# A language-model layer on one core: the router's product folded into the projection, and another opening

## The chip, the core and the metric

One Trainium2 core runs the whole program in one launch. It has five instruction streams: TensorE (PE, matrix products into PSUM), VectorE (DVE), ScalarE (ACT), GpSimd (POOL) and SyncE (SP, which here issues DMAs), all in order, each waiting on semaphores that the others or the DMAs raise. The metric is the device time of one execution in microseconds (us).

## The reference

128 sequences of 128 tokens, width 128. The layer is one embedding, one attention and one mixture of experts:

```python
nesting, segments = _syntax_info(token_ids)
combined = concat([pos_emb, nest_table[nesting], seg_table[segments]])   # [b, s, 384]
h = combined @ W                                                         # width 128
h = h + attention(layernorm(h))       # 8 heads of 64, causal inside the 128 tokens, biases on q, k, v, o
x2 = layernorm(h)
logits = x2 @ router_w.T + router_b   # 8 experts
top 2 of logits, softmax over the two -> weights
h = h + sum over the two experts of weight * (fc2(silu(h1) * h2) + b)    # h1, h2 = split(x2 @ fc1 + b), 2 * 256
```

Positions come from a table, and nesting and segment codes from comparisons and running sums over the token ids. The layer norms have no scale or shift.

## The kernel before

**Stages.** An opening loads the weights, computes codes from the token ids, writes them to DRAM and reads them back spread over 72 partitions, builds a table of embeddings (`code_table`), splits the projection weights into a high part and a rest (`w_hi`, `w_lo`) and prepares two groups of four sequences. Then sixteen octets of eight sequences run attention and routing, software-pipelined: in each turn k of an octet (one sequence), `octet_steps` lists the steps that every engine then works off in the same order, each engine picking the kinds it has a part in. The last octet is followed by `last_steps`, which drains the routing of the last groups. The rows of all tokens are scattered to DRAM by expert, and an expert phase in blocks of 256 rows follows, once for the first choice and once for the second.

**A turn.** With n = k mod 4 the turn holds: scores (L1113), a query, a value and a key product for the next group, each as three products of high and low parts (L1050 to L1052), softmax (mask and row maximum on DVE L809 and L813, exponentials on ACT L640 in two halves of four heads, scaling of one half on POOL L497 and of the other on DVE L826), transposes of the probabilities (L1120, L1125), mix with the values (L1137) and projection (L1147), whose result DVE adds to `residual` as `h2` (L837). The embedding (n=0, L1065), its norm and transposes (n=1, n=2) of the group two ahead are put between.

**Routing of a group, over four turns.** DVE takes statistics of `h2` (n=2) and writes the normalised rows `normed2` (n=3, L857). In the n=0 turn PE transposes the rows (L1155) and ACT copies them to `x2T` (L632); in n=1 PE multiplies them with `w_router` (L1164, 8 columns), DVE adds the bias (L863) and takes the two largest; n=2 makes one-hots of the choices; n=3 ranks them (L1172, L1173); n=0 turns ranks into row numbers, and POOL scatters (L529) in n=0 and n=1. The PSUM banks KEY and VALUE are shared by these steps with the key and value products, so the next product waits until they have been read out.

**The opening's order.** SP first raises all counting semaphores by 64 (so that waits can count backwards), then issues x, the embedding tables, wq, wk, wv, their biases, wo, the two halves of the expert weights w1 (1 MB each, into the still unused `kT[1]` and `qT[1]`), w2, the router's weight, b2 and b1, and only then waits for the codes and stores them. `first_steps` does embedding, norm and transposes of group 0, then of group 1, then query, value and key of group 0 four times. Before the first octet ACT casts both halves of w1 (L663) and DVE computes their rest (L994); ACT waits for that rest before it goes on.

## Time and profile before

| what | value |
|---|---|
| median of 3 runs | 1486.12 us (1485.44 to 1490.86) |
| profiled execution | 1479.45 us, span 1477.7 us |
| PE, DVE, ACT, POOL busy over the span | 88%, 81%, 72%, 60% |
| granted TensorE clock, mean | 0.973 |
| opening, to the first scores | 0 to 60 us |
| attention with routing | 60 to 1042 us |
| expert phase | 1050 to 1478 us |

The shares are averages over stages with different limits. A row of the chain of waits gives the start, the length and the work that the end of the program hangs on at that time; a row of the windows gives for each engine how long it was busy in that stretch. Idle time of an engine that nothing waits for costs nothing.

### The profile page before, as it was taken

To read this page: it belongs to the slowest core of one execution; us is meant where nothing else is said; L and a number is where in the kernel's file an instruction comes from. 1 tells how busy PE (TensorE), PEld (TensorE's weight loads), DVE (VectorE), ACT (ScalarE), POOL (GpSimd) and SP (SyncE) were. 2 spreads that over 40 slices of the span, in tenths; PEclk is the share of its full clock that TensorE was granted. 3 is DMA by queue.
4 is the path that set the end of the run, shared out by engine and by line. 5 is a ranking of instruction groups with operands and counts; after the bars stand their busy time and mean duration, and the time that the engine had idled before them with its cause. 6 is when DMAs were issued, how large, how long until landed. Compare 5 with 4: busy or idle time off the path is not lost.

```text
span 1477.7 us, 42129 instructions
## 1 busy us (share of the span) xinstructions
PE 1300.5 (88%) x11234; PEld 1128.5 (76%) x11235; DVE 1195.4 (81%) x3683; ACT 1057.6 (72%) x3382; POOL 889.5 (60%) x1161
## 2 busy tenths in 40 slices
PE   1699999999999999999999999993399999699996
PEld 0488777777777777777777777773399999699996
DVE  4478888888888888888888888884588888588885
ACT  0599888888888888888888888882255555355553
POOL 3134566656665666566656665666366767477775
PEclk9999999999999999999999999996699999899998
DMA  4042111101110111011101110111789999899995
GB/s 150 3 175 79 33 46 39 40 31 45 38 40 31 45 38 40 31 45 38 40 31 45 38 40 31 45 38 57 248 306 343 345 337 340 278 335 346 338 348 187
DMA packets 91501, 188.43 MB, mean 128 GB/s; under 512 B 18404, under 2 KB 38588, under 8 KB 90812
## 3 DMA queue, kind: packets, MB, share of 16 engines
q1 hardware_dynamic: 50748, 66.35, 14.7%
q10 hardware_dynamic: 20864, 76.87, 13.6%
q0 software_dynamic: 19840, 44.62, 8.6%
q8 instruction: 23, 0.38, 0.1%
q14 instruction: 26, 0.21, 0.1%
HBM read 50.40 MB, written 57.44 MB: 73 GB/s over the span
## 4 chain that ended last, share of the span: by engine, by line
PE 33%; DVE 19%; issue 16%; ACT 12%; DMA 10%; POOL 6%; SPq 2%; DVEq 1%; ACTq 0%; POOLq 0%
ACT probs L640 6%; PE ps L1137 6%; PE ps L1147 4%; PE ps L1050 3%; DMA v<-xs 3%; ACT v L627 3%; PE ps L1052 3%; PE ps L1051 3%; DVE neg_max L813 3%; PE ps L1202 3%; DVE masked L809 3%; DVE probsT L817 2%; ACT qT L618 2%; PE ps L1164 2%; PE ps L1120 2%
## 5 line engine op out<-in xcount | busy, mean ns | idle before, releaser
L640 ACT ACTIVATE probs<-masked,neg_max 128x128 f32<-128x128 f32 x1024 | 398.5, 393 | 9.9 <-DVE neg_max L813 8.0
L529 POOL DMA_INDIRECT xs<-normed,row x256 | 266.1, 1039 | 79.7 <-issue 72.4
L497 POOL TENSOR_TENSOR probs<-probs,inv_sums 128x512 f32<-128x512 f32 x128 | 133.0, 1039 | 268.0 <-DVE inv_sums L821 267.9
L640 ACT ACTIVATION_READ_ACCUMULATOR probs<-masked,neg_max 128x1 f32 x1024 | 193.8, 189 | 0.0
L809 DVE TENSOR_TENSOR masked<-ps,causal 128x1024 f32<-128x1024 f32 x128 | 155.7, 1216 | 37.7 <-PE ps L1113 36.1
L1050 PE MATMUL ps<-xT_hi,w_now 128*128 128x256 f32 x576 | 178.8, 310 | 6.8 <-issue 6.1
L1137 PE MATMUL ps<-probsT,v 128*64 128x128 f32 x2048 | 140.2, 277 | 35.2 <-DVE probsT L817 35.2
L594 ACT ACTIVATE masked<-ps,w_now 128x256 f32<-128x256 f32 x288 | 120.7, 470 | 65.0 <-PE ps L1052 55.1
L1051 PE MATMUL ps<-xT_lo,w_now 128*128 128x256 f32 x576 | 163.3, 283 | 0.0
L1052 PE MATMUL ps<-xT_hi,w_now 128*128 128x256 f32 x576 | 163.2, 283 | 0.0
L986 DVE SCALAR_TENSOR_TENSOR probsT<-ps,w_now,masked 128x256 f32<-128x256 f32 x288 | 126.1, 480 | 41.7 <-PE ps L1052 21.6
L1202 PE MATMUL ps<-w,probsT 128*128 x1152 | 152.2, 275 | 3.6 <-DVE probsT L986 3.6
L813 DVE TENSOR_REDUCE neg_max<-masked 128x8 f32<-128x1024 f32 x128 | 154.9, 1210 | 0.0
L1137 PEld LDWEIGHTS ps<-probsT,v 128*64 128x64 f32 x2048 | 113.0, 137 | 54.8 <-issue 45.5
L1113 PE MATMUL ps<-kT,qT 64*128 64x128 f32 x2048 | 149.7, 286 | 0.8 <-ACT kT L621 0.8
L1202 PEld LDWEIGHTS ps<-w,probsT 128*128 128x128 f32 x1152 | 141.1, 192 | 4.2 <-issue 4.2
L1113 PEld LDWEIGHTS ps<-kT,qT 64*128 64x128 f32 x2048 | 125.0, 188 | 22.9 <-issue 21.7
L563 POOL DMA_INDIRECT xs<-probs,v x108 | 104.9, 971 | 61.2 <-DVE probs L967 31.2
L1147 PE MATMUL ps<-w_o,mixedT 128*128 128x128 f32 x1024 | 136.2, 276 | 0.0
L563 POOL DMA_INDIRECT out_h<-probs,v x108 | 104.5, 968 | 51.9 <-issue 28.2
L578 ACT CAST xT_hi<-ps 128x256 fp32r<-128x256 f32 x144 | 53.6, 372 | 103.4 <-PE ps L1182 100.8
L1147 PEld LDWEIGHTS ps<-w_o,mixedT 128*128 128x128 f32 x1024 | 125.3, 193 | 0.0
(190 smaller groups left out, 3264.9 us busy)
## 6 DMA issues: line engine op xcount, KB each, us to landing
w_now<-w_parts ACTq DMA_DIRECT2D x144, 514.0 KB
v<-xs SPq DMA_DIRECT2D x108, 260.0 KB
kT<-xs SPq DMA_DIRECT2D x36, 260.0 KB
normed<-h SPq DMA_DIRECT2D x32, 256.0 KB, 2.6
pads<-pad_rows SPq DMA_DIRECT2D x8, 520.0 KB, 2.8
xs<-pad_rows SPq DMA_DIRECT2D x8, 520.0 KB, 3.6
xs<-normed,row POOLq DMA_INDIRECT x256, 2.4
xs<-pads SPq DMA_DIRECT2D x12, 260.0 KB
```

The lines of the kernel that those rows point to most:

```text
L529: pool.indirect_dma_start((xs[0], xs_parts)[k], bass.IndirectOffsetOnAxis(ap=row[par][:, k, j:j + 1].bitcast(U32), axis=0), normed2[par][: ...
L563: pool.indirect_dma_start((xs_parts, out)[k], bass.IndirectOffsetOnAxis(ap=xt[j][:, r, GOES_TO[k]:GOES_TO[k] + 1].bitcast(U32), axis=0), y ...
L640: ins = nc.scalar.activation(probs[par][:, n], masked[par][:, n], ACT.Exp, bias=neg_max[par][:, n:n + 1], scale=1.0, accum_out=sums[par][: ...
L809: V.tensor_tensor(masked[par][:], ps[:, SCORES:SCORES + 2].rearrange("p a (n k) -> p (a n) k", n=4), causal[:].unsqueeze(1).broadcast_to([ ...
L813: V.tensor_reduce(neg_max[par][:], masked[par][:], AX, ALU.max, negate=True).then_inc(max_ready, 1)
L1050: T.matmul(dst, w_hi_, x_hi_, start=True, stop=False)
L1051: T.matmul(dst, w_hi_, x_lo_, start=False, stop=False)
L1052: return T.matmul(dst, w_lo_, x_hi_, start=False, stop=True)
L1113: ins = T.matmul(ps[:, SCORES + e, pair * S:(pair + 1) * S], qT[gp][rows, pair, cols], kT[gp][rows, pair, cols], start=True, stop=True)
L1137: ins = T.matmul(ps[e * HD:(e + 1) * HD, MIX, pair * S:(pair + 1) * S], v[gp][:, j, head * HD:(head + 1) * HD], probsT[:, e * PAIRS + pair ...
L1147: ins = T.matmul(ps[:, QUERY, 0:D], mixedT[:, n], w_o[:, n], start=(n == 0), stop=(n == PAIRS - 1))
L1202: ins = T.matmul(ps[:, YB[z], r * D:(r + 1) * D], actT[z][:, half, r * S:(r + 1) * S], w2[:, bass.ds(e * 2 * D + half * D, D)], start=(hal ...
```

## The change

Two edits that share tiles.

**The router's product.** Let w_c be the router's weight with the mean over the 128 features taken off (`centre` @ `w_router`). Then the router's logits of a row are rstd times (h2 @ w_c) plus the bias. h2 is linear in table rows, mixed values and biases, so w_c is multiplied into the embedding weights, `w_o` and the output bias once, as 8 more columns (D2 = 136). `code_table`, `pos_emb`, `w_o`, `bias_o`, `h`, `residual` and `h2` get 136 columns. The projection then yields the raw logits with no product of their own; the embedding gets a second narrow product (`embed_r`, n=1). The steps `route_normT` and `route_logits` go; in the n=3 turn DVE scales the raw logits by rstd and adds the bias.

**The opening.** The semaphores are raised by PE and ACT, half each. SP issues x, the router's weight, transposed copies of W and wo, the tables and the projection weights, then the codes. ACT issues w1 first thing, and b1, the router bias, w2 and b2 after its cast of `w_hi`. DVE makes `part_code` and `part_mask` ahead of the codes. `first_steps` weaves group 1's embedding, norm and transposes between the query, value and key products of group 0. The cast of w1 moves to ACT's part of the eight turns of octet 0 and its rest to POOL's part of octet 1.

```diff
             steps.append(("embed", half + 2))
         elif n == 1:
-            late("route_logits", half - 2)
+            steps.append(("embed_r", half + 2))
...
-            late("route_normT", half - 2)
             steps.append(("stats", half + 2))
             late("route_rows", half - 3)
         elif n == 1:
@@ -98,6 +98,9 @@
             steps.append(("residual", half + 1))
         if octets_done == 0:
             steps.extend(("pad", n) for n in ((2 * k, 2 * k + 1) if k < GB else (GB + k,)))
+            steps.append(("w1_hi", k))
+        if octets_done == 1:
+            steps.append(("w1_lo", k))
...
-            [(w, 0, n) for n in range(PAIRS) for w in ("query", "value", "key")])
+    steps = [(w, 0) for w in ("onehot", "embed", "embed_r", "stats", "rstd")] + [("split", 0), ("onehot", 1)]
+    steps += [(w, 0) for w in ("norm", "normT", "xlo")] + [("bias", 0)]
+    between = {0: [("embed", 1)], 1: [("embed_r", 1)], 2: [("normT", 1)], 3: []}
+    behind = {0: [("stats", 1), ("rstd", 1)], 1: [("norm", 1)], 2: [("xlo", 1)], 3: [("onehot", 2), ("residual", 0)]}
+    for n in range(PAIRS):
+        steps += [(w, 0, n) for w in ("query", "value", "key")] + between[n] + behind[n]
```

SP's loads, POOL's and ACT's share, the router's steps on DVE, and PE's opening with the narrow product:

```diff
-            for s in led:
-                sp.sem_inc(s, LEAD)
             sp.dma_start(x_raw[:], a["x"]).then_inc(s_x, 16)
+            sp.dma_start(w_router[:], a["wr"]).then_inc(s_wr, 16)
+            sp.dma_start(w_embT[:], a["w_embT"]).then_inc(s_wrT, 16)
+            sp.dma_start(w_oT[:], a["woT"]).then_inc(s_wrT, 16)
+            sp.dma_start(bias_oT[:], a["boT"]).then_inc(s_wr, 16)
...
             sp.dma_start(bias_vT[:], a["bv"]).then_inc(s_wqkv, 16)
-            sp.dma_start(bias_o[:], a["bo"].broadcast_to([128, D])).then_inc(s_wqkv, 16)
-            sp.dma_start(w_o[:], a["wo"].rearrange("(c p) n -> p c n", c=PAIRS)).then_inc(s_wqkv, 16)
-            sp.dma_start(w1_raw[0][:].rearrange("p a b -> p (a b)"), a["w1"][:, 0:EXPERTS * FC1 // 2]).then_inc(s_w1, 16)
-            sp.dma_start(w1_raw[1][:].rearrange("p a b -> p (a b)"), a["w1"][:, EXPERTS * FC1 // 2:]).then_inc(s_w1, 16)
-            sp.dma_start(w2[:], a["w2"]).then_inc(s_w1, 16)
-            sp.dma_start(w_router[:], a["wr"]).then_inc(s_w1, 16)
-            sp.dma_start(bias_r[:], a["br"].broadcast_to([S, EXPERTS])).then_inc(s_w1, 16)
-            sp.dma_start(b2_all[:], a["b2"].broadcast_to([S, EXPERTS * D])).then_inc(s_w1, 16)
-            sp.dma_start(b1_all[:].rearrange("p e c -> p (e c)"), a["b1"]).then_inc(s_b1, 16)
+            sp.dma_start(bias_o[:, 0:D], a["bo"].broadcast_to([128, D])).then_inc(s_wqkv, 16)
+            sp.dma_start(w_o[:, :, 0:D], a["wo"].rearrange("(c p) n -> p c n", c=PAIRS)).then_inc(s_wqkv, 16)
...
+                elif kind == "w1_lo":
+                    pool.wait_ge(s_w1hi, i + 1)
+                    pool.tensor_tensor(w1_parts[:, i, FC1:2 * FC1], w1_parts[:, i, FC1:2 * FC1].bitcast(F32),
+                                       w1_parts[:, i, 0:FC1].bitcast(F32), ALU.subtract).then_inc(s_w1lo, 1)
...
+            for s in led[0::2]:
+                act.sem_inc(s, LEAD)
+            act.dma_start(w1_parts[:, :, FC1:2 * FC1].bitcast(F32), a["w1"].rearrange("p (e c) -> p e c", e=EXPERTS)).then_inc(s_w1, 16)
+            act.wait_ge(s_ext_ps, 1)
+            act.wait_ge(s_w, 16 * 4)
+            nc.scalar.copy(w_emb[:, :, D:D2], ps[:, KEY, EXPERTS:4 * EXPERTS].rearrange("p (c e) -> p c e", c=3)).then_inc(s_ext, 1)
+            nc.scalar.copy(w_o[:, :, D:D2], ps[:, KEY, 4 * EXPERTS:8 * EXPERTS].rearrange("p (c e) -> p c e", c=PAIRS)).then_inc(s_ext, 1)
             act.wait_ge(s_wqkv, 16 * 8)
             nc.scalar.mul(bias_q8[:], bias_qk[:, 0], HD ** -0.5).then_inc(s_whi, 1)
             nc.scalar.copy(w_hi[:], w_raw[:]).then_inc(s_whi, 1)
+            act.dma_start(w1_parts[:, :, 2 * FC1:W1ROW].bitcast(F32), a["b1"].rearrange("p (e c) -> p e c", e=EXPERTS)).then_inc(s_b1, 16)
+            act.dma_start(bias_r[:], a["br"].broadcast_to([S, EXPERTS])).then_inc(s_w2, 16)
+            act.dma_start(w2[:], a["w2"]).then_inc(s_w2, 16)
+            act.dma_start(b2_all[:], a["b2"].broadcast_to([S, EXPERTS * D])).then_inc(s_w2, 16)
...
+                elif kind == "embed_r":
+                    dve.wait_ge(embed_r_full, LEAD + G + 1)
+                    V.tensor_tensor(h[par][:, :, D:D2], ps[:, VALUE, 0:GB * EXPERTS].rearrange("p (j e) -> p j e", j=GB),
+                                    pos_emb[:, D:D2].unsqueeze(1).broadcast_to([S, GB, EXPERTS]), ALU.add).then_inc(embedded_r, 1)
...
-                    dve.wait_ge(x2T_full, LEAD + G - 1)
+                    V.tensor_tensor(raw[:], h2[par][:, :, D:D2], rstd2[:].unsqueeze(2).broadcast_to([S, GB, EXPERTS]), ALU.mult).then_inc(raw_ready, 1)
...
-                    dve.wait_ge(logits_full, LEAD + G + 1)
+                    dve.wait_ge(raw_ready, LEAD + G + 1)
                     dve.wait_ge(top_at_ready, LEAD + G)
-                    V.tensor_tensor(logits[:], ps[:, VALUE, 0:GB * EXPERTS].rearrange("p (j e) -> p j e", j=GB),
+                    V.tensor_tensor(logits[:], raw[:],
                                     bias_r[:].unsqueeze(1).broadcast_to([S, GB, EXPERTS]), ALU.add).then_inc(logits_ready, 1)
...
+            for s in led[1::2]:
+                pe.sem_inc(s, LEAD)
+            pe.wait_ge(s_centre, 1)
+            pe.wait_ge(s_wr, 32)
+            T.matmul(ps[:, KEY, 0:EXPERTS], centre[:], w_router[:], start=True, stop=True).then_inc(s_wc_ps, 1)
+            pe.wait_ge(s_wc, 1)
+            pe.wait_ge(s_wrT, 32)
+            for c in range(3):
+                T.matmul(ps[:, KEY, (1 + c) * EXPERTS:(2 + c) * EXPERTS], w_embT[:, c * 128:(c + 1) * 128], w_c[:], start=True, stop=True)
+            for c in range(PAIRS):
+                ins = T.matmul(ps[:, KEY, (4 + c) * EXPERTS:(5 + c) * EXPERTS], w_oT[:, c * 128:(c + 1) * 128], w_c[:], start=True, stop=True)
+            ins.then_inc(s_ext_ps, 1)
             pe.wait_ge(s_w, 16 * 4)
-            T.matmul(ps[:, VALUE, 0:D], posT[:], w_emb[:, 0], start=True, stop=True, skip_group_check=True)
-            T.matmul(ps[0:CODES, VALUE, D:2 * D], nestT[:], w_emb[:, 1], start=False, stop=False, skip_group_check=True)
-            T.matmul(ps[0:CODES, VALUE, D:2 * D], segT[:], w_emb[:, 2], start=False, stop=True, skip_group_check=True).then_inc(s_table_ps, 1)
+            pe.wait_ge(s_ext, 1)
+            T.matmul(ps[:, VALUE, 0:D2], posT[:], w_emb[:, 0], start=True, stop=True, skip_group_check=True)
+            T.matmul(ps[0:CODES, VALUE, D2:2 * D2], nestT[:], w_emb[:, 1], start=False, stop=False, skip_group_check=True)
+            T.matmul(ps[0:CODES, VALUE, D2:2 * D2], segT[:], w_emb[:, 2], start=False, stop=True, skip_group_check=True).then_inc(s_table_ps, 1)
+            pe.wait_ge(s_bias_v, 1)
+            pe.wait_ge(s_ext, 2)
+            pe.wait_ge(s_wc, 2)
+            for n in range(PAIRS):
+                T.matmul(ps[:, MIX, 0:D2], bias_v[:, n], w_o[:, n], start=(n == 0), stop=False)
+            T.matmul(ps[:, MIX, D:D2], bias_oTs[:], w_c[:], start=False, stop=True).then_inc(s_bias_o_ps, 1)
...
+                elif kind == "embed_r":
+                    if first:
+                        pe.wait_ge(embedded, LEAD + G + 1)
+                    else:
+                        pe.wait_ge(v_ready, LEAD + GB * (G - 1) + 2)
+                    for j in range(GB):
+                        ins = T.matmul(ps[:, VALUE, j * EXPERTS:(j + 1) * EXPERTS], onehot[:, j * S:(j + 1) * S], code_table[:, D:D2],
+                                       start=True, stop=True)
+                    ins.then_inc(embed_r_full, 1)
```

Value products wait for the woven steps:

```diff
                 elif kind == "value":
...
                     elif j == 1:
                         pe.wait_ge(embedded, LEAD + G + 2)
                     elif j == 2:
-                        pe.wait_ge(logits_ready, LEAD + G - 2)
+                        pe.wait_ge(embedded_r, LEAD + G + 2)
                     else:
                         pe.wait_ge(xlo_ready, LEAD + G + 2)
```

Where instructions stand. PE, from right behind an n=0 turn's mix of probabilities and values into the n=1 turn (scores, nine products of query, value and key, the step behind them), before:

```order
L1155 MATMUL ps<-ident,normed_0 128x128 x4
L1113 MATMUL ps<-kT,qT 128x128 x8
L1050 MATMUL ps<-xT_hi,w_hi 128x512
L1051 MATMUL ps<-xT_lo,w_hi 128x512
L1052 MATMUL ps<-xT_hi,w_lo 128x512
L1050 MATMUL ps<-w_hi,xT_hi 128x512
L1051 MATMUL ps<-w_lo,xT_hi 128x512
L1052 MATMUL ps<-w_hi,xT_lo 128x512
L1050 MATMUL ps<-xT_hi,w_hi 128x512
L1051 MATMUL ps<-xT_lo,w_hi 128x512
L1052 MATMUL ps<-xT_hi,w_lo 128x512
L1164 MATMUL ps<-w_router,x2T 128x8 x4
```

and now, from the mix (`ps<-probsT,v`) on:

```order
L1180 MATMUL ps<-probsT,v 64x128 x8
L1156 MATMUL ps<-kT,qT 128x128 x8
L1085 MATMUL ps<-xT_hi,w_hi 128x512
L1086 MATMUL ps<-xT_lo,w_hi 128x512
L1087 MATMUL ps<-xT_hi,w_lo 128x512
L1085 MATMUL ps<-w_hi,xT_hi 128x512
L1086 MATMUL ps<-w_lo,xT_hi 128x512
L1087 MATMUL ps<-w_hi,xT_lo 128x512
L1085 MATMUL ps<-xT_hi,w_hi 128x512
L1086 MATMUL ps<-xT_lo,w_hi 128x512
L1087 MATMUL ps<-xT_hi,w_lo 128x512
L1109 MATMUL ps<-code_table,onehot 128x8 x4
```

The transposes L1155 ahead of the scores are gone, and the router's product L1164 behind the value and key products has become four narrow products of table and one-hot.

DVE in the n=3 turn, from the copy of the ranks to the maximum of the next turn (`gap_one` and `normed` behind it are the routing weights), before:

```order
L902 COPY ranks<-ps 128x128
L817 COPY probsT<-ps 128x512
L837 TENSOR_TENSOR h_0<-ps,residual 128x128
L779 TENSOR_SCALAR onehot<-code_rows,part_code 72x512
L857 TENSOR_SCALAR normed_1<-h_1,moments,rstd 128x128 x4
L894 TENSOR_SCALAR gap_one<-gap_exp 128x4
L896 RECIPROCAL normed_0<-gap_one 128x4
L898 TENSOR_TENSOR normed_0<-gap_exp,normed_0 128x4
L821 RECIPROCAL inv_sums<-sums 128x4
L809 TENSOR_TENSOR masked<-ps,causal 128x1024
```

and now:

```order
L927 COPY ranks<-ps 128x128
L843 COPY probsT<-ps 128x512
L863 TENSOR_TENSOR h_0<-ps,residual 128x136
L795 TENSOR_SCALAR onehot<-code_rows,part_code 72x512
L881 TENSOR_TENSOR raw<-h_1,rstd 128x32
L883 TENSOR_SCALAR normed_1<-h_1,moments,rstd 128x128 x4
L888 TENSOR_TENSOR logits<-raw,bias_r 128x32
L919 TENSOR_SCALAR gap_one<-gap_exp 128x4
L921 RECIPROCAL normed_0<-gap_one 128x4
L923 TENSOR_TENSOR normed_0<-gap_exp,normed_0 128x4
L847 RECIPROCAL inv_sums<-sums 128x4
L835 TENSOR_TENSOR masked<-ps,causal 128x1024
```

Two operations of 32 columns stand on either side of the four norms; the bias add was behind the n=1 turn's maximum before.

SP's loads at the start, from wo (`w_o`) to the first codes that come back, before:

```order
L330 DMA w_o<-in_wo 128x4x128
L331 DMA kT<-in_w 128x2048
L332 DMA qT<-in_w 128x2048
L333 DMA w<-in_w 128x2048
L334 DMA w_router<-in_wr 128x8
L335 DMA bias_r<-in_br 128x8
L336 DMA b_all<-in_b 128x1024
L337 DMA b_all<-in_b 128x32
L340 DMA codes<-v 128x2x128
L341 DMA codes<-v 16x2x128
L347 DMA code_rows<-codes 48x512
```

and now:

```order
L339 DMA bias_o<-in_bo 128x128
L340 DMA w_o<-in_wo 128x4x128
L343 DMA codes<-v 128x2x128
L344 DMA codes<-v 16x2x128
L350 DMA code_rows<-codes 48x512
```

The seven loads between wo and the store of the codes are gone from this queue.

## Rows read from the trace of the kernel before

Columns of the windows: stretch, length, then busy us and count for PE, PEld, DVE, ACT and POOL, the granted clock, the DMA share and GB/s.

**Rows 1.** Windows of one steady group: us, then PE, PEld, DVE, ACT, POOL busy, clock, DMA.
```profile
300.25:307.63 7.38, 7.33 (x66) 6.15 (x65) 5.37 (x14) 6.19 (x22) 5.53 (x7) 1.00 0.10 36
...
321.63:329.84 8.21, 7.23 (x68) 5.87 (x66) 7.80 (x24) 6.70 (x22) 3.00 (x6) 1.00 0.00 0
300.25:329.84 29.59, 28.01 (x252) 23.09 (x251) 25.82 (x82) 25.78 (x88) 18.45 (x25) 1.00 0.12 38
```

**Rows 2.** Windows, first octet: the group of sequences 4 to 7, and its n=1 turn.
```profile
89.54:115.80 26.26, 25.93 (x239) 21.82 (x237) 21.82 (x53) 24.55 (x85) 10.97 (x22) 1.00 0.48 179
...
96.50:102.72 6.22, 6.22 (x60) 5.34 (x58) 5.18 (x14) 5.97 (x21) 3.29 (x7) 1.00 0.35 131
```

**Rows 3.** Groups by line and shape, 300 to 420 us: busy us, mean ns | idle before.
```profile
L497 POOL TENSOR_TENSOR probs<-probs,inv_sums 128x512 f32<-128x512 f32 x17 | 17.7, 1039 | 35.7 <-DVE inv_sums L821 35.7
...
L1147 PE MATMUL ps<-w_o,mixedT 128*128 128x128 f32 x128 | 16.9, 275 | 0.0
...
L1164 PE MATMUL ps<-w_router,x2T 128*128 128x8 f32 x32 | 4.2, 259 | 0.2
...
L632 ACT COPY x2T<-ps 128x512 f32<-128x512 f32 x5 | 2.9, 585 | 0.2
...
L1065 PE MATMUL ps<-code_table,onehot 72*128 72x128 bf16 x16 | 1.6, 221 | 0.5
...
L863 DVE TENSOR_TENSOR logits<-ps,bias_r 128x32 f32<-128x32 f32 x4 | 0.8, 192 | 0.9 <-PE ps L1164 0.9
```

**Rows 4.** Chain that ended last, steady group: start, us, what.
```profile
313.80 0.17 DVE h L837
...
328.23 1.09 PE ps L1137 x16
329.32 0.60 PE ps L1155 x4
...
330.42 1.55 ACT probs L640 x7
...
333.34 1.06 PE ps L1164 x8
```

**Rows 5.** The same chain over the opening.
```profile
6.78 1.15 SPq L319
...
19.09 10.12 DMA codes<-v
...
31.47 0.36 DVE onehot L779
...
39.86 0.35 DVE onehot L779
...
49.33 0.80 PE ps L1050
...
60.06 1.16 PE ps L1113 x16
...
64.04 2.28 DVE w_parts L994
66.33 1.15 DVE masked L809
```

**Rows 6.** Timeline of the opening: start, us, instruction [idle before, releaser].
```profile
9.54 0.23 DVE L719 CAST v<-v 128x128 f32<-128x128 int32 x1 [9.54 <-DMA v<-in_x]
...
14.83 0.23 DVE L735 CAST v<-v 128x128 bf16<-128x128 int32 x1
...
36.31 1.12 DVE L800 TENSOR_SCALAR normed<-h,moments,rstd 128x128 f32<-128x128 f32 x4 [1.60 <-POOL rstd L468]
...
59.91 1.89 ACT L663 CAST w_parts<-kT 128x2048 fp32r<-128x2048 f32 x1
```

**Rows 7.** The chain again, behind attention.
```profile
1009.54 1.09 POOL xs L529
...
1041.91 7.67 DMA xs<-normed,row
```

176 lines of the change are left out of this document (77 added, 99 removed).

## The prediction

> **What bounds the kernel now.** I read the table of windows first, because the busy shares of the whole span mix an opening, sixteen octets of attention and an expert phase. One steady group of four sequences takes 29.59 us; in it TensorE is busy 28.01 us, VectorE 25.82 and ScalarE 25.78 [rows 1]. A turn (one sequence) with little idle on TensorE is the n=1 turn, 7.33 of 7.38 us; in the n=0 turn VectorE is the full one, 7.80 of 8.21, and TensorE has a microsecond of idle time in it. A group of the first octet, which has no router transposes, products, ranks or scatters yet, takes 26.26 us [rows 2]: routing costs 3.33 us a group, and that is the ceiling of anything won from it.
>
> Next the chain of waits through a steady group. From 313.80 to the mix product at 328.23 it is VectorE's almost without a gap (some forty pieces, one stretch of POOL among them), then on TensorE and ScalarE: mix, the router's transposes (L1155), ScalarE's exponentials at 330.42, the value copy, the router's product (L1164) [rows 4]. So both of TensorE's router steps stand on the chain; the VectorE half of the chain is full, and whatever is added there lengthens it.
>
> Then the opening, as the chain of the first 70 us [rows 5]. SyncE's first DMA is issued at 6.78, behind its semaphore increments. The codes are ready at 15.06 [rows 6], but their two stores stand behind all weight loads; the second is issued at 19.09 and has landed 10.12 us later. The first one-hot starts at 31.47, the first query product at 49.33 (two groups prepared one behind the other), the first scores at 60.06. VectorE splits the expert weights until 66.3 and takes the scores only then. Everything up to there is nearly pure latency: a microsecond taken off is one microsecond of the end.
>
> Last the tail. After attention the chain is POOL's: a row of scatters from 1009.54, then the last landing at 1041.91 [rows 7]. The last two groups' router steps lie under those scatters, so I give the change nothing there. The expert phase behind it runs the same instructions on the same weights: nothing either.
>
> **The router's fold, per steady group.** Removed from TensorE on the chain: the transposes, 0.60 us [rows 4]. ScalarE's copy of the transposed rows (0.585 [rows 3]) goes too, but the mixedT copy of about the same length runs beside the transposes, so only one of the two lengths is won: from the end of mix at 329.32 the exponentials can start after one copy, at about 329.85 in place of 330.42 [rows 4], 0.57 us. The product goes, 4.2 us over four groups, 1.05 a group; the new narrow product of one-hot and table's last 8 columns takes its place, and its nearest row is the same product at 128 columns, 1.6 over four groups, 0.40 [rows 3]: 0.65 us won. Fewer columns are not worth less time here: the router's own product has 8 columns and 259 ns, the projection 128 columns and 275 [rows 3]. Together 1.22.
>
> Added: two small VectorE operations (scaling the raw logits by rstd, and the bias add, which moves from the n=1 turn) in the n=3 turn, inside the full half of the chain. The bias add is 192 ns [rows 3]; two of them are 0.38 at most, and 0.1 at least, since small operations overlap in issue. I take 0.30. The new add from PSUM in the n=1 turn replaces the old bias add of the same size: nothing. The projection gets 8 more columns: 16.9 us over 128 instructions (each two passes and 16 sequences) [rows 3], so at most 8/128 of 1.06 us, 0.07 a sequence, at least nothing; four times, on the chain for two of four turns: 0 to 0.14, taken 0.10. The wider residual and h2 adds: 8/128 of small operations, 0.05. Net 1.22 - 0.30 - 0.10 - 0.05 = 0.77 us a group, bounds 0.4 (all additions full, some of the win filled by VectorE) and 1.25. Both router steps occur for 30 groups before the tail: **23 us, 12 to 38**.
>
> **The opening.** Semaphore increments leave SyncE, so x is issued at about 0.4 instead of 6.78, lands some 2.8 us later (9.54 against 6.78 [rows 5, 6]), but VectorE first waits for the router's folded weight: constants from POOL, five DMAs (20 issues took from 7.93 to 19.09, so 0.56 us each), their landing, one product: done at about 6.9. The code computation takes 5.5 us (9.54 to 15.06 [rows 6]): codes at 12.5. SyncE has by then issued its 17 loads (the first 1.15 us, the rest 0.56 each, done near 10.5) and issues the second store at 13.1, not 19.09. What the store costs is the open point: 10.12 us before with 3.5 MB of weights ahead in its queue [rows 5]. Now the 2 MB of w1 is issued by ScalarE at about 3.6 us and should be through by 13, and w2 and b2 (1.5 MB) are issued after the store. Lower bound 2.5 us for the store (x took 2.8), upper bound the old 10. I take 3, since little is left in flight, then 2.3 for the loads (29.21 to 31.47 before): first one-hot at **18.5**, between 17.5 and 22 (the ends are 2.5 and some 6.5 us of store; the full 10 is a rival). The table chain on VectorE ends near 16 and is covered.
>
> From one-hot to the first query was 8.5 us for one group (31.47 to 39.9, the second group used 39.9 to 49.33 [rows 5]). Now 0.95 more for the narrow product and its add ahead of the statistics, and 0.55 because the weight split (1536 columns, where 2048 take 2.28 [rows 5]: 1.7) and the next one-hot (0.35) are put into the 1.60 us in which VectorE waited for POOL's rstd [rows 6]: 10.0 us. The query block took 10.7 (49.33 to 60.06). With the second group woven in, value 1 waits for the embed add (0.9), value 2 for the narrow add and the transposes for the norm (about 0.6), value 3 for the low part of x (1.5): 13.7, between 12 and 15.5. First scores at 18.5 + 10.0 + 13.7 = 42.2, not 60.06: 17.8 won. The stall behind the expert split, 66.33 against 61.2 where the scores ended, goes: 4.5 (3.2 to 5.5; the low end if TensorE's own work in the first two turns is what is late next).
>
> Given back: eight ScalarE casts of 128x512 in octet 0, a quarter each of the 1.89 us row [rows 6], 0.47; ScalarE is nearly full there (24.55 of 26.26 [rows 2]), so between 0 and 0.47 a turn: 2.5 in all (0 to 4). POOL's eight subtractions in octet 1, near 1.04 each like the 128x512 product [rows 3], beside idle time of POOL: 0.5 (0 to 2). The narrow product in octet 0, where TensorE is full: 0.5. Opening: 17.8 + 4.5 - 2.5 - 0.5 - 0.5 = **18.8 us, 11 to 26**.
>
> **Sum.** 18.8 + 23.1 = 41.9 us off the profiled execution's own 1479.45, which gives 1437.5. The runs shown have their median 6.7 us higher, at 1486.12; taken off that, 1444.2. I forecast 1444.
>
> **A rule against a row.** For the store, the table of the opening shows that a DMA behind 3.5 MB on one queue lands after 10.12 us. The Trainium skill (DMA: Bandwidth & Descriptors, Issuing engines are not separate DMA queues) says DMAs issued by several engines run on the same 16 engines and interleave, so issuing w1 from ScalarE saves only sequencer time. By the rule the codes still share bandwidth with w1 and w2; the sum would be 3 to 4 us smaller. No run here shows it yet.
>
> **Rivals.** (A) VectorE takes over as the bound. VectorE has 25.82 us of work and gets 0.4 more; its chain half is already without gaps. If its backlog fills what TensorE gives up, the fold is worth 0 to 0.3 us a group and only the opening stays: 1486 - 19 - 5 = 1462. For it: the 14 us without a gap. Against it: 3.77 us of VectorE idle in each group, 2.01 of them in turn n=1 [rows 1], where the larger win falls. The Trainium skill (Perfetto Trace Analysis, Identifying the Most-Contended Engine) says to judge TensorE by weight-load busy share, not by matmuls; that is 23.09 us a group here, below VectorE's, and the rule speaks for this rival. (B) Both steps pay in full and the VectorE additions hide: 1.25 a group, 38 us, with the opening 57: 1429. (C) The codes still queue: the store lands as late after its issue as before, first one-hot at 25, opening 12 rather than 19: 1451 with the fold. (D) Slower: the additions on VectorE (0.38), the narrow product (0.40), its add (0.19) and the wide columns (0.28 over four turns) are paid in full, 1.25 us a group on 32 groups, 40 us, while the removed steps were only fillers of waits for VectorE. With the opening that is 1486 + 40 - 19 = 1507. It decides from the point where the n=1 and n=0 turns do not shrink and the group passes 30.2 us. Against it: the n=1 turn has TensorE at 99%, and the same turn without router steps took 6.22 us in octet 0 [rows 2]. (E) The change does not do what it says at the opening (VectorE waits at the router weight or the full load of q, k, v until after the codes are there): part of C.
>
> **Chances.** Forecast 0.55 (1434 to 1454 is its own range); A 0.17; B 0.13; C with E 0.11; D 0.04. The range should hold 8 in 10: from 1422 (B with a good opening) to 1464 (A). The measurement tells 0.5%, 7.4 us, from no change. Faster by more: everything but D and the poorest part of A, 0.93; within: 0.04; slower: 0.03.
>
> **What would show it.** First one-hot near 18.5 and first scores near 42; no wait of VectorE's mask for the expert split. Steady group near 28.8 us, n=1 near 6.7, n=0 near 7.7, n=3 about 0.3 longer. The n=1 turn of octet 0 some 0.5 longer than 6.22. Wrong if the store takes over 6 us, if a steady group is still above 29.3 or below 28.3, or if the expert phase changes its length.

## The result and the profile after

The changed kernel takes **1444.02 us** (median of four runs, 1441.04 to 1446.21) beside 1487.19 for the kernel before (four runs, 1485.44 to 1490.86) on the same chip: a ratio of 0.9705 with the 95% interval 0.9677 to 0.9733. Its profiled execution took 1442.6 us, span 1440.8. Repeated later in another session it took 1441.25 us beside 1485.13, ratio 0.971 [0.9694, 0.9726].

The forecast was 1444. Its parts were not as good as its sum, and the rest of this text is about that. The table cuts the span at four points that both traces show: the first scores, the scores of the ninth sequence (behind the first octet), the scores of the last sequence, and the first transpose of the expert phase. All in us.

| stretch | before (three profiles) | after (two profiles) | difference of the means |
|---|---|---|---|
| start to first scores | 60.06, 61.39, 59.49 | 48.53, 47.36 | -12.4 |
| first two turns | 16.40, 15.71, 16.45 | 11.95, 11.92 | -4.3 |
| other six turns of the octet | 39.34, 39.38, 39.32 | 41.88, 41.90 | +2.5 |
| the next 120 turns | 878.09, 878.24, 877.86 | 846.07, 846.22 | -31.9 |
| last scores to expert phase | 60.77, 60.39, 60.27 | 60.64, 60.74 | +0.2 |
| expert phase | 423.0, 428.8, 433.4 | 431.7, 428.6 | +1.7 |

The 120 turns repeat within 0.4 us and the six turns within 0.1; the very start moves by a microsecond or two with the first loads. The expert phase is the same program in both kernels and scatters by 10 us from execution to execution. So small effects can be read from the cut points and not from the end. In the first two turns the kernel before also has a lower granted clock (0.79, 0.89 and 0.79, against 1.00 in both profiles after), so a part of the -4.3 came through the clock.

Windows of the changed kernel: the first two turns, the other six of the first octet, then an n=1 turn, an n=0 turn and the whole of a steady group. The columns are those of [rows 1, 2].

```profile
48.53:60.48 11.95, 9.40 (x83) 7.23 (x83) 9.52 (x23) 9.32 (x32) 2.62 (x6) 1.00 0.12 45
60.48:102.36 41.88, 39.61 (x360) 32.94 (x358) 31.77 (x72) 39.40 (x134) 12.97 (x32) 1.00 0.44 162
280.76:287.34 6.58, 6.51 (x63) 5.36 (x62) 5.72 (x19) 6.12 (x21) 4.74 (x5) 1.00 0.06 20
301.36:309.28 7.92, 6.89 (x63) 5.46 (x62) 7.66 (x20) 6.21 (x21) 3.07 (x6) 1.00 0.00 0
280.76:309.28 28.52, 26.91 (x244) 21.93 (x243) 26.67 (x83) 25.23 (x86) 18.89 (x25) 1.00 0.12 40
```

Against [rows 1] the n=1 turn went from 7.38 to 6.58 us, the n=0 turn from 8.21 to 7.92, the group from 29.59 to 28.52. Over all 120 turns the mean n=1 turn went from 7.38 to 6.58, n=0 from 8.21 to 7.80, n=2 from 6.93 to 7.15 and n=3 from 6.98 to 6.91. TensorE works 1.10 us less in a group, VectorE 0.85 more: VectorE now has 26.67 of 28.52. The lengths of most groups alternate in both kernels (29.43 and 29.62 before, 28.32 and 28.47 after), on the mean of the two 29.53 and 28.40.

The chain through the steady group, to be laid beside [rows 4]: the router's raw product and its scaling on VectorE (L881, L888), mix (L1180), the exponentials, the narrow product (L1109), the projection (L1190).

```profile
300.77 0.18 DVE raw L881
...
302.02 0.10 DVE logits L888
...
308.26 1.11 PE ps L1180 x16
...
309.87 1.54 ACT probs L656 x7
...
312.78 0.26 PE ps L1109 x4
...
313.96 0.93 PE ps L1190 x8
```

From the start of mix to the exponentials it is 1.61 us, where it was 2.19 [rows 4]: the transposes are gone and one copy is left. Between the value copy and the attention's transposes stands a product of 0.26 us, where the router's took 1.06. In return 0.18 and 0.10 us of VectorE are on the chain.

By line and shape, 280 to 395 us, the answer to [rows 3]:

```profile
L1190 PE MATMUL ps<-w_o,mixedT 128*128 128x136 f32 x128 | 17.5, 279 | 0.0
...
L1109 PE MATMUL ps<-code_table,onehot 72*128 72x8 bf16 x16 | 1.0, 169 | 0.3
...
L881 DVE TENSOR_TENSOR raw<-h,rstd 128x32 f32<-128x32 f32 x4 | 0.7, 180 | 0.0
L888 DVE TENSOR_TENSOR logits<-raw,bias_r 128x32 f32<-128x32 f32 x4 | 0.7, 178 | 0.0
```

The opening's chain, to be laid beside [rows 5]. "issue" is time in which the trace shows nothing that is waited for.

```profile
2.67 2.63 DMA v<-in_boT
5.30 2.87 issue
8.17 0.58 PE ps L1061 x2
...
8.85 0.17 DVE w_c L749
...
15.00 3.68 DMA codes<-v
...
19.09 4.01 DMA code_rows<-codes
...
23.29 0.36 DVE onehot L795
...
33.78 0.76 PE ps L1085
```

The last of the constants is there at 5.30, but TensorE's first product starts at 8.17: it is still issuing its half of the semaphore increments. The codes are ready at 14.54, the second store is issued at 15.00 and lands in 3.68 us, where it took 10.12 [rows 5]; their loads take 4.01, where they took 1.66 in the trace of before. From the store's landing to the first one-hot, the issue of the loads included, it is 4.61 us, where it was 2.26. First one-hot 23.29 (31.47 before), first query product 33.78 (49.33), first scores 48.53 (60.06). The mask behind the first scores no longer waits for a split of expert weights, as it did from 61.2 to 66.33 [rows 5].

### The profile page after: what moved, and what is told of

It reads as the page before. It is cut to its first block, busy times and chain, and to the rows that moved or that the text cites. A ratio compares the mean times of both kernels' runs of the same rounds, so it can differ in the third digit from the quotient of the medians.

```text
span 1440.8 us, 41566 instructions
## 1 busy us (share of the span) xinstructions
PE 1269.9 (88%) x11004; PEld 1093.6 (76%) x11005; DVE 1206.8 (84%) x3749; ACT 1039.4 (72%) x3358; POOL 906.6 (63%) x1171
## 4 chain that ended last, share of the span: by engine, by line
PE 31%; issue 19%; DVE 18%; ACT 14%; DMA 8%; POOL 8%; SPq 1%; DVEq 0%; POOLq 0%; ACTq 0%
ACT probs L656 7%; PE ps L1180 6%; PE ps L1190 4%; DVE neg_max L839 4%; PE ps L1085 3%; ACT v L648 3%; ACT qT L639 3%; PE ps L1227 3%; DMA v<-xs 3%; PE ps L1087 3%; PE ps L1086 3%; PE ps L1163 2%; DVE probsT L843 2%; POOL xs L537 2%; PE ps L1168 2%
## 5 line engine op out<-in xcount | busy, mean ns | idle before, releaser
L537 POOL DMA_INDIRECT xs<-normed,row x256 | 260.2, 1016 | 79.7 <-issue 68.3
L835 DVE TENSOR_TENSOR masked<-ps,causal 128x1024 f32<-128x1024 f32 x128 | 155.7, 1216 | 23.3 <-PE ps L1156 10.9
L1180 PE MATMUL ps<-probsT,v 128*64 128x128 f32 x2048 | 140.9, 279 | 32.2 <-DVE probsT L843 29.1
L1180 PEld LDWEIGHTS ps<-probsT,v 128*64 128x64 f32 x2048 | 113.0, 137 | 52.4 <-issue 46.1
L1190 PE MATMUL ps<-w_o,mixedT 128*128 128x136 f32 x1024 | 141.8, 282 | 0.8 <-ACT mixedT L676 0.8
L1190 PEld LDWEIGHTS ps<-w_o,mixedT 128*128 128x128 f32 x1024 | 129.4, 192 | 1.1 <-issue 1.1
```

The source lines that it names most:

```text
L537: pool.indirect_dma_start((xs[0], xs_parts)[k], bass.IndirectOffsetOnAxis(ap=row[par][:, k, j:j + 1].bitcast(U32), axis=0), normed2[par][: ...
L835: V.tensor_tensor(masked[par][:], ps[:, SCORES:SCORES + 2].rearrange("p a (n k) -> p (a n) k", n=4), causal[:].unsqueeze(1).broadcast_to([ ...
L1180: ins = T.matmul(ps[e * HD:(e + 1) * HD, MIX, pair * S:(pair + 1) * S], v[gp][:, j, head * HD:(head + 1) * HD], probsT[:, e * PAIRS + pair ...
L1190: ins = T.matmul(ps[:, QUERY, 0:D2], mixedT[:, n], w_o[:, n], start=(n == 0), stop=(n == PAIRS - 1))
```

## The experiments

Twelve kernels ran. Seven undo or add one thing in the changed kernel, one combines four of them, one takes its whole opening back, and three are the two kernels themselves again. Four of them (incs_pool, w2_later, split_early, logits_n1) went to another chip, on which the kernel before takes 1669.64 us; more on it under logits_n1. The times of these four are not compared with the first chip's, only their openings, with logits_n1 as the base, since that one leaves the opening as it is.

### The fold without the opening

The old opening comes back (SyncE raises the semaphores, big weights ahead of the codes, groups one behind the other, expert weights split ahead of the octets):

```diff
+            for s in led:
+                sp.sem_inc(s, LEAD)
...
+            sp.dma_start(w1_parts[...], a["w1"]...).then_inc(s_w1, 16)   # and b1, br, w2, b2, ahead of the codes
...
-            act.dma_start(w1_parts[...], a["w1"]...).then_inc(s_w1, 16)
...
-    between = {0: [("embed", 1)], 1: [("embed_r", 1)], 2: [("normT", 1)], 3: []}
+    steps += [(w, 1) for w in ("embed", "embed_r", "stats", "rstd", "norm", "normT", "xlo")] + ...
```

> The fold kept, the old opening put back: semaphores raised by SyncE, all expert loads on SyncE ahead of the codes, group 1 behind group 0, expert weights split before the first octet (the fold's own small loads and products stay). If the steady saving is the fold's, the groups stay near 28.4 us and the time is that of before less 30 to 34 us, 1454 to 1457, with the first scores near 61 us. If the steady saving came with the other opening (other addresses, transfers or phase), the groups go back toward 29.5 us and the time is above 1475.

Measured: 1460.18 us (1453.88 to 1460.74) beside 1484.59, ratio 0.9823 [0.9791, 0.9856], 3 us above what was expected. Windows of the opening and of the 120 turns:

```profile
0.00:66.52 66.52, 22.42 (x93) 18.01 (x94) 23.06 (x86) 12.18 (x21) 17.25 (x50) 1.00 0.30 91
123.97:970.32 846.35, 799.69 (x7203) 652.50 (x7201) 777.31 (x2432) 751.58 (x2558) 544.55 (x732) 1.00 0.12 41
```

The 120 turns take 846.35 us, as in the changed kernel (846.07, 846.22), so the whole -31.9 is the fold's and none of it the opening's. The opening alone shows something that the sum had not priced whole: with the fold and the old order the first scores come at 66.52, 6 us later than before and 5.5 later than expected. The first one-hot is at 34.99 (31.47), since SyncE's queue reaches the second store at 24.39 instead of 19.09: one issue in it, that of the router bias behind w1 and b1, lasts 5.89 us (at most 0.97 for any issue between x and the store in the kernel before). So this opening is not quite the old one. From the one-hot to the query are 20.07 us, where it was 17.86: in each group 0.44 for the narrow product and its add (1.16 from the add of the embedding to the statistics, where it was 0.72), and 1.3 where GpSimd's var_eps runs beside the weight split (more under split_early). To the ninth sequence it is 123.97 us, 8.2 more than before: of the fold's 31.9 us, 24 are left in the whole kernel with this opening. With the new opening the ninth sequence comes at 101.2 to 102.4.

### The kernel before, again

> The kernel before, unchanged, profiled once more. The profiled execution of before had 423.0 us from the first transpose of the expert phase to the end, that of after 430.6, with the same instructions. If this is scatter from one execution to the next, this profile shows an expert phase that differs from 423.0 by several us, while its attention stage agrees with the first profile within 1 us (60.1 to 993.9). If the change lengthened the expert phase, this one is within 1.5 us of 423.0.

1485.8 us, span 1483.9, 6 us longer than the first profile. The expert phase starts at 1055.11 (1054.66 in the first), the first scores being 1.3 us later and the first two turns 0.7 shorter; the expert phase itself took 428.8 us instead of 423.0. That is the scatter of the table.

### Big weights ahead of the codes on SyncE's queue

```diff
+            sp.dma_start(w1_parts[...], a["w1"]...); b1; bias_r; w2; b2     # SyncE, behind all its other loads
...
-            act.dma_start(...)                                              # the same five on ScalarE
```

> The changed kernel with w1, b1, router bias, w2 and b2 issued by SyncE ahead of the store of the codes, nothing else undone. If the place in the queue is what made the store slow before, the landing of the store goes from 3.7 us back to about 10 and the first one-hot from 23.3 to 28 to 30 us. If only bytes in flight count and not the queue, the weights are through by the time of the store and the one-hot stays at 22 to 24.

1446.97 us in one run. Its opening chain:

```profile
10.36 5.50 SPq L343
...
17.32 7.56 DMA codes<-v
...
25.28 1.75 DMA code_rows<-codes
...
27.23 0.36 DVE onehot L795
```

The second store is issued at 17.32, not 15.00, and lands in 7.56 us, not 3.68: 6.2 us together, of which 2.3 come back because nothing is in flight beside the codes' loads (1.75, not 4.01). The later issue is not the price of five more issues: one of them, the router bias (L343), holds SyncE for 5.50 us, where the same issue on ScalarE takes 0.68 behind a landed w1; why is not shown. First one-hot 27.23, 3.9 us later than in the changed kernel's first profile (5.4 than in its second) and somewhat less than expected.

What this run does not separate is the queue from the bytes in flight. The weights were not through by the time of the store, as the second half of the expectation needed: w1 was issued at 8.89 and landed at 19.45 (4.20 and 16.55 in the changed kernel), and w2 and b2 were issued at 15.90 and 16.37, ahead of the store (18.94 and 19.41, behind it, in the changed kernel), and landed at 21.92 and 24.46. With w1 on ScalarE's queue a store issued earlier, at 12.99, took 4.23 us (incs_pool) and 4.92 (all_new), where one at 15.00 took 3.40 to 4.01. Big loads issued later and ahead of the store would explain the 7.56 on any queue.

### The second group not woven in

```diff
-    between = {0: [("embed", 1)], 1: [("embed_r", 1)], 2: [("normT", 1)], 3: []}
-    behind = {0: [("stats", 1), ("rstd", 1)], 1: [("norm", 1)], 2: [("xlo", 1)], 3: [("onehot", 2), ("residual", 0)]}
+    steps += [(w, 1) for w in ("embed", "embed_r", "stats", "rstd", "norm", "normT", "xlo")] + [("onehot", 2), ("residual", 0)]
```

> The changed kernel with group 1's embedding, norm and transposes put back ahead of the query, value and key products of group 0. The prediction priced the weaving at 9.4 us of a second group saved against 3.0 of waits put into the products. If so the first scores move from 48.5 to 54 to 55.5 us. If the woven steps cost the products as much as they saved, they stay within 2 us of 48.5.

1452.07 us in one run. First one-hot 21.96, first scores 53.31: 31.35 us between them, where the changed kernel has 25.24 and, in its second profile, 25.56. The first scores are a little ahead of what was expected, because the one-hot was 1.3 us earlier; from one-hot to scores the weaving is worth 5.8 to 6.1 us, and the terms of the sum give 6.4 (9.4 for the second group, less 3.0 for the longer block).

### TensorE's increments on GpSimd

```diff
+            for s in led[1::2]:
+                pool.sem_inc(s, LEAD)
...
-            for s in led[1::2]:
-                pe.sem_inc(s, LEAD)
```

> The changed kernel with TensorE's half of the semaphore increments moved to POOL behind its constants. In the profile TensorE's first product starts at 8.14 us although the last load it needs had landed at 5.3. If its own increments held it, it starts at 5.4 to 6 now, the codes are ready some 2.5 us earlier (near 12) and the first one-hot starts 1.5 to 2.8 us earlier than 23.3. If another wait held it, the product stays near 8.1.

The opening chain of this kernel (the other chip; logits_n1 there has 8.16, 14.99 and 22.18 at the same three places):

```profile
5.48 0.58 PE ps L1061 x2
...
12.99 4.23 DMA codes<-v
...
20.34 0.36 DVE onehot L797
```

The first product starts right behind the last constant, the codes' store is issued 2.0 us earlier, and the first one-hot comes 1.8 earlier. So the 2.87 us of "issue" in the changed kernel's chain were TensorE's own increments.

### Small weights behind the first codes

```diff
+            act.wait_ge(codes_in[0], LEAD + 32)
+            act.wait_ge(codes_in[1], LEAD + 32)
             act.dma_start(w1_parts[:, :, 2 * FC1:W1ROW]...)      # b1, then br, w2, b2
```

> The changed kernel with b1, router bias, w2 and b2 issued only when the first two loads of codes are in. If w2 and b2 in flight made the loads of the codes take 4.0 us instead of the 1.7 of before, the first one-hot moves from 23.3 to 20.5 to 21.5 us. If the load's time is its own, it stays within 0.5 us.

```profile
15.00 4.00 DMA codes<-v
...
19.41 1.66 DMA code_rows<-codes
...
21.26 0.36 DVE onehot L797
```

The store is unchanged (4.00), the loads take 1.66 us. With w2 and b2 (1.5 MB from ScalarE's queue) in flight the same loads took 2.34 to 4.16 us in the seven traces that have them (2.82 in logits_n1), so what it won here is 0.9 us of the first one-hot (22.18 in logits_n1) and up to 2.5 elsewhere. A queue of its own did not keep these small loads from a big one.

### The low half of the weights, earlier

```diff
-                elif kind == "split":
-                    V.tensor_tensor(w_lo[:], w_raw[:], w_hi[:].bitcast(F32), ALU.subtract)
...
+            V.tensor_tensor(w_lo[:], ...)          # ahead of the first one-hot
```

> The changed kernel with the rest of the projection weights computed on VectorE while it waits for the codes, not between group 0's statistics and norm. POOL's first operation of rstd took 1.53 us beside that split, 0.24 without it. If the split slows POOL, that operation is back at 0.24 and the span from one-hot to the first query product shrinks from 10.5 to 9.0 to 9.4 us. If the split is hidden there, the span stays within 0.3 of 10.5.

First one-hot 23.16, query 32.51: 9.35 us, where it is 10.49 in the changed kernel and 10.48 in logits_n1. What was in the way there is GpSimd's var_eps, which this timeline of the changed kernel shows beside VectorE's split:

```profile
26.96 1.72 DVE L825 TENSOR_TENSOR w_lo<-qT,w_hi 128x1536 fp32r<-128x1536 f32 x1
27.24 1.53 POOL L469 TENSOR_SCALAR var_eps<-moments 128x4 f32<-128x4 f32 x1 [12.58 <-DVE moments L814]
```

The same instruction takes 0.23 us in split_early, where VectorE's split has been done by 20.7. Beside VectorE's 128x1536 subtraction, then, GpSimd's small operation pays 1.3 us.

### Raw and logits in the n=1 turn

```diff
-                    V.tensor_tensor(raw[:], h2[par][:, :, D:D2], rstd2[:]..., ALU.mult).then_inc(raw_ready, 1)
...
+                elif kind == "route_logits":       # two turns later, GpSimd waits for raw_ready ahead of the next rstd
+                    V.tensor_tensor(raw[:], h2[par][:, :, D:D2], rstd2[:]..., ALU.mult).then_inc(raw_ready, 1)
```

> The changed kernel with the scaling of the raw logits and the bias add moved out of the n=3 turn, ahead of the maximum in the n=1 turn. If they stand on the chain there at 0.28 us a group, the group falls from 28.4 to about 28.1 us and the time by some 8 us, 1435 to 1438. If VectorE is as full in the n=1 turn now, or they were covered, the group stays within 0.1 us and the time at 1444.

**Inconclusive, and the one surprise against the result.** 1688.04 us (1682.28 to 1690.74), before there 1669.64 (1667.47 to 1671.24): a ratio of 1.0104 [1.0078, 1.013]. The other three took 1683.61, 1684.5 and 1685.64 on that chip, one run each: all four variants of the changed kernel are about 1% slower there than the kernel before. Their common part is the change itself. The trace shows two differences from the first chip. The expert phase takes 555 us instead of 430, at 241 GB/s and a DMA share of 0.70, not 310 and 0.90, and a granted clock of 0.92, not 0.96. And nearly each steady group has one stretch like this one (timeline, steady group):

```profile
275.77 1.09 PE L1183 MATMUL ps<-probsT,v 128*64 128x128 f32 x16
...
276.79 1.16 PE L1159 MATMUL ps<-kT,qT 64*128 64x128 f32 x16
...
279.72 0.59 ACT L678 COPY mixedT<-ps 128x512 f32<-128x512 f32 x1 [3.11 <-remote]
279.88 1.22 DVE L837 TENSOR_TENSOR masked<-ps,causal 128x1024 f32<-128x1024 f32 x1 [0.83 <-remote]
```

The mix ends at 276.86 in the records of TensorE, and ScalarE's copy of it starts at 279.72, with "remote", a releaser that the trace does not know. Between 110 and 1040 us there are 26 such waits of ScalarE, 89.5 us together; the traces of the first chip have none in either kernel. All four traces of the second chip have 26 of them, 89.1 to 89.5 us, all in the n=2 turn, one in each group from the fourth to the thirtieth but the eighteenth. That turn takes 10.9 to 11.3 us there on the mean, not 7.15, and the other three turns differ from the changed kernel's on the first chip by 0.2 at most. A fixed place in each group is what the rival of before_third says, though for the kernel before it stays untested. Behind it TensorE has little to do for 2 us, and then the granted clock is 0.50 for some 3.5 us:

```profile
270.21:302.53 32.32, 28.44 (x244) 23.32 (x242) 26.09 (x83) 25.16 (x86) 18.15 (x25) 0.95 0.11 36
...
283.50:285.50 2.00, 2.00 (x11) 2.00 (x10) 0.42 (x1) 1.13 (x3) 1.42 (x2) 0.50 0.10 33
```

The group takes 32.32 us. There is no profile of the kernel before on that chip, so whether it has fewer of these stretches stays open; its mean granted clock there is 0.950 to 0.958, against 0.934 to 0.937 for logits_n1, which says that something of the kind differs, not what. An estimate from the times: the kernel before is 184.5 us slower there than on the first chip; if its expert phase loses the same 125 us, some 60 are left for everything ahead of it, where the 120 turns alone of logits_n1 take 122 us more than the changed kernel's on the first chip.

### The kernel before, the third time

> The kernel before, unchanged, profiled beside the next three. On the chip of the four runs ahead of this one (before 1669.64 us, changed kernels 1683 to 1688) the steady groups of logits_n1 hold 26 idle stretches, one in nearly every group, in which mixedT on ScalarE waits 3.4 us on the mean for a product whose records end long before (89.5 us in all), and behind each the granted clock lies at 0.5 for some 3.5 us; the profile of the changed kernel on the first chip has none. If this run comes to such a chip, one theory says that the stretches come with how densely TensorE is fed, and then before has fewer or shorter ones, some 15 to 20 with 50 to 65 us in all, and that makes the changed kernel slower there. The rival says that the chip has them at a fixed place of each group in any kernel: 26 of them with 85 to 95 us here too, and then the 1 per cent must come from elsewhere. If it comes to a chip like the first: 1480 to 1489 us, no such stretch, and the run says only how far the expert phase scatters (423.0 and 428.8 us in the two profiles so far).

It came to the first chip: 1488.62 us, no such stretch, expert phase 433.4 us. The question about the second chip stays open.

### The changed kernel, again

> The changed kernel, unchanged, on the same chip as the other three. On a chip like the first: 1441 to 1447 us, ratio to before 0.968 to 0.973, steady groups 28.3 to 28.5 us, first one-hot 23 to 24 us. On a chip like the second: 1683 to 1690 us and a ratio of 1.007 to 1.012, by what the four variants of it gave there.

1441.25 us (1438.53 to 1443.51), ratio 0.971 [0.9694, 0.9726]; steady groups 28.33 and 28.48 us, as expected. The first one-hot came at 21.80, ahead of the 23 to 24 expected: the codes' loads took 2.48 us, not 4.01.

### Expert weights split ahead of the octets

```diff
-            steps.append(("w1_hi", k))
-        if octets_done == 1:
-            steps.append(("w1_lo", k))
...
+            for n in range(2):                     # ScalarE copies, VectorE subtracts, ahead of the first turn
+                nc.scalar.copy(w1_parts[:, es, 0:FC1], ...); V.tensor_tensor(w1_parts[:, es, FC1:2 * FC1], ...)
```

> The expert weights split ahead of the first octet again (ScalarE 2 copies, VectorE 2 subtractions, before the first attention turn), all else of the changed kernel kept. By the terms of the sum the stall of 4.5 us in the first two turns comes back and the 2.5 + 0.5 us of the later turns go: the first two turns 15.5 to 16.5 us (11.95 in the changed kernel), the six after them 39 to 40 (41.88), the scores of k=8 1.5 to 2.5 us later. The rival says that in the woven opening the split finds engines idle before the first scores (VectorE 12.4 of 20 us busy from 40 to 60) and costs 2 us at most there: first two turns 12 to 14 us, six after them 39 to 40, k=8 0 to 2 us earlier than in the changed kernel.

Windows of early_w1, then of the changed kernel (after_again): first two turns, other six.

```profile
47.15:63.87 16.72, 11.70 (x83) 9.07 (x83) 13.84 (x25) 12.46 (x33) 2.96 (x5) 0.80 0.09 32
63.87:103.82 39.95, 39.36 (x361) 32.97 (x359) 31.55 (x71) 37.29 (x128) 13.86 (x32) 1.00 0.45 164
```

```profile
47.36:59.28 11.92, 9.38 (x83) 7.23 (x83) 9.51 (x23) 9.31 (x32) 2.62 (x6) 1.00 0.12 45
59.28:101.18 41.90, 39.64 (x360) 32.93 (x359) 31.79 (x72) 39.44 (x134) 12.96 (x32) 1.00 0.44 162
```

The stall comes back, 4.80 us in the first two turns, a part of it through the clock (0.80 against 1.00), and 1.95 us of the six others go: 2.85 us for the late split. The 120 turns are the same (846.56), so GpSimd's subtractions in octet 1 cost nothing that shows. The rival, a split that finds idle engines, falls. The times of the whole kernels don't show it (1437.88, one run, its expert phase 424.6 us): this is the size that only the cut points resolve.

### Four edits together

```diff
+                pool.sem_inc(s, LEAD)                           # as incs_pool
+            act.wait_ge(codes_in[1], LEAD + 32)                 # as w2_later
+            V.tensor_tensor(w_lo[:], ...)                       # as split_early
+                elif kind == "route_logits":                    # as logits_n1
```

> Four edits on the changed kernel at once: TensorE's increments issued by GpSimd (one-hot 2.9 us earlier in incs_pool), b1, br, w2, b2 issued behind the first codes (1 to 1.5 us earlier in w2_later), w_lo split ahead of the first one-hot (one-hot to query 1.1 us shorter in split_early), and raw and logits moved out of the n=0 turn into the n=1 turn. One theory says that the n=1 turn has room on VectorE (5.72 of 6.58 us) and that 0.28 us goes from VectorE's chain of the n=0 turn: 8.4 us over 30 groups, with the opening's 4.5 some 13 us, ratio to after_again 0.99. The rival says that TensorE is the bound of a whole group by now (26.91 of 28.52 us) and the room is used elsewhere: steady groups as in after_again within 0.1 us, and the opening's 4.5 us alone, ratio 0.997. Of the opening both expect the first one-hot at 18.5 to 20, the query at 28 to 29.5, the first scores at 43 to 45 us.

**1435.01 us** (1432.47 to 1439.67), ratio to before 0.9657 [0.9641, 0.9673], the fastest of all. The 120 turns take 843.31 us, not 846.22, and the steady groups 28.12 and 28.31 instead of 28.33 and 28.48: 0.19 us in most groups, between the 0.28 of the one theory and the nothing of the other. Over the 120 turns it is 2.9 us, 0.10 a group, since some groups are longer than in the changed kernel (28.66 instead of 28.45, 28.68 instead of 28.14). The opening missed: the first one-hot came at 20.73, not by 20. The second store, issued at 12.99 while w1 was in flight until 16.50, took 4.92 us, and w_lo now stands ahead of the one-hot and had to wait for the load of the weights (VectorE's split 19.06 to 20.8). First scores 45.32 against 47.36; but the ninth sequence's scores came at 101.46, later than the 101.18 of the changed kernel. Windows show where the gain went, all_new from its second turn and then the same stretch of after_again:

```profile
49.07:56.20 7.13, 4.62 (x39) 3.54 (x38) 6.03 (x17) 6.87 (x26) 2.54 (x5) 0.94 0.14 55
56.20:62.50 6.30, 6.28 (x38) 5.32 (x39) 3.29 (x9) 4.21 (x17) 1.60 (x5) 0.52 0.41 154
```

```profile
51.10:58.23 7.13, 4.62 (x39) 3.54 (x38) 6.03 (x18) 6.88 (x26) 2.54 (x5) 1.00 0.15 57
58.23:62.50 4.27, 4.25 (x41) 3.46 (x41) 2.70 (x8) 3.99 (x17) 1.31 (x3) 1.00 0.43 161
```

The first stretch is the same work in the same 7.13 us, TensorE 4.62 us busy in both, with idle times of 1.66 and 0.87 us in it. In all_new the granted clock falls to 0.50 within the second of them, at 55.4, and stays there for some 7 us; in after_again it stays at 1.00. From there to the fourth turn all_new takes 10.64 us, after_again 8.33: 2.3 us. serial and queue_old fell as well (first eight turns 56.18 and 56.16 us, all_new 56.14), the two profiles of the changed kernel did not (53.83, 53.82). serial and queue_old differ from the changed kernel in their openings alone, so a change of the opening can tip it; what decides is not shown. The fall costs more than most of the edits made here won.

## Why the prediction was right, point by point

- **What bounds.** Right: both router steps stood on the chain, the turns without them are shorter, and the opening was latency. The profile's 1478 us of before fell to 1441.
- **Transposes and copy, 0.57 a group.** 0.58 (2.19 to 1.61).
- **The product, 1.05 to 0.40.** The win was put too small. The narrow product takes 0.26 on the chain, so 0.80 was won, not 0.65. The step that failed is "fewer columns are not worth less time here": it took the row at 128 columns, 0.40, as the price of 8. That held for the two fp32 products compared (259 and 275 ns), not for the bf16 one, whose row at 128 columns lasts 1.6 us over 16 and at 8 columns 1.0.
- **Raw and logits, 0.30 on the chain.** 0.28 by the rows; moving them to the n=1 turn won 0.10 a group over the 120 turns (all_new). The n=3 turn did not get 0.3 longer, as the signs had it: it is 6.91, where it was 6.98, and the n=2 turn is 0.22 longer.
- **Wider projection 0.10, wider adds 0.05.** L1190 takes 279 ns in place of 275 and 0.93 or 0.94 on the chain where it was 0.91: 0.03 a piece. The add is 295 ns instead of 287. Both next to nothing.
- **The fold in all, 0.77 a group, 23 us.** By the measured terms 0.58 + 0.80 - 0.28 - 0.03 = 1.07, and 31.9 us over the 30 groups is 1.06. The turns agree: 0.80 of it is won in the n=1 turn, where the product stood, and 0.26 in the other three. Inside the bounds (0.4 to 1.25) and above the value taken; the product's 0.15 and the additions' 0.14 are the difference.
- **First one-hot at 18.5.** The largest miss: 23.29, outside of its own 17.5 to 22 (21.80 to 21.96 in after_again, serial and early_w1, at its upper end). Three terms. The second store was issued at 15.00 instead of 13.1, since TensorE's half of the increments was priced at nothing and its product came 2.0 us late. The store took 3.68 instead of 3; w1, which was to be through by 13, landed at 16.55. From landing to one-hot it was 4.61 instead of the 2.3 of before, since the codes' loads took 4.01 and not 1.66. incs_pool shows the first and w2_later the last; the store's 0.7 is not taken apart. The increments had been seen in the trace as SyncE's 6.4 us; that a share of them moves to the engine that has the first product to make was the thing not asked.
- **One-hot to query 10.0.** 10.49. The narrow product and its add cost 0.44, not 0.95; the split put beside GpSimd's work cost more than its 0.55, since it made var_eps 1.3 us longer: split_early has 9.35.
- **Query block 13.7.** 14.75, within 12 to 15.5. The gain of the weaving was 5.8 to 6.1, not 6.4.
- **The stall, 4.5.** 4.3 on the mean in the table (3.8 to 4.5), 4.80 by early_w1. It is not VectorE's split alone, as the prediction had it: the lower clock is in it.
- **Given back: 2.5 and 0.5 for the splits, 0.5 for the narrow product in octet 0.** 2.5 in all: 1.95 for the casts in octet 0, 0.6 left for the fold (39.95 in early_w1, 39.34 before), and nothing in octet 1.
- **The opening in all, 18.8.** 13.4 in the first pair of profiles (115.80 to 102.36), 14.1 on the mean: inside 11 to 26, low. The first scores were to come 17.8 earlier and came 11.5.
- **Tail and expert phase, nothing.** +0.2 us in the tail; the expert phase scatters by 10 us in both kernels and shows no shift beyond that.
- **Sum 41.9.** To the start of the expert phase 45.6 in the first pair (1054.66 to 1009.07), 43.2 by the medians of the runs. The opening's 5 us too many and the fold's 9 too few cancelled to within 4. The rest is the expert phase's scatter: by the cut points of all five profiles the change is worth 45.8 us ahead of that phase, by the medians of the runs 43.2 and 43.9. The mechanisms hold, but that the median came out at 1444.02 is luck, and the prediction's number is better than its reasons.

**The rivals.** A (VectorE takes over, the fold is worth nothing) falls: the group lost 1.06 us on the mean while VectorE's work rose to 26.67 of 28.52. The Trainium skill's rule to judge TensorE by its weight-load share (Perfetto Trace Analysis, Identifying the Most-Contended Engine) put VectorE first and spoke for A (its other measure, the share of peak FLOPs, is not worked out here); here steps taken from TensorE, with one copy of ScalarE, made the group 1.07 to 1.13 us shorter while VectorE got more to do, so the trace does not bear it out. B's 38 us for the fold was nearer than the forecast's 23 by little: 31.9 lies between. C is half true: the store did not queue as before (3.68 against 10.12), and yet the first one-hot was late for three other reasons, and C's 12 us for the opening is nearer to the measured 13.4 to 14.1 than the forecast's 18.8. D falls with the n=1 turn at 6.58.

**The rule on queues.** First the rows: the same store took 10.12 us before, 7.56 with the big weights ahead on its own queue, 3.68 with them on ScalarE's; and the codes' loads took 1.66 us with nothing in flight and 4.01 with w2 on the other queue. The Trainium skill (DMA: Bandwidth & Descriptors, Issuing engines are not separate DMA queues) says that the engines underneath are shared, and by it the sum was to be 3 to 4 us smaller. The store came 0.7 us over its term and the stretch behind it 2.3, 3.0 together, so the trace agrees with its direction and with the lower end of its size; in after_again the two are 0.7 and 0.8. Whether the place in one's own queue counts beside that is not shown, since queue_old changed the bytes in flight as well.
